# One-hot rows in one VectorE instruction, earlier negated means, and squares of incoming rows spread one, two, one: attention, routing and eight experts on one core

## What is computed

```python
x = x + jnp.tanh(g_xattn[0]) * attention(layernorm(x), ctx, ctx, lens, lens, W, b)
x = x + jnp.tanh(g_ffn[0]) * experts(layernorm(x), router_w, w_gate, w_up, w_down)

# attention: softmax(Q K^T / 16, masked) V W^T + b, with K = V = ctx, 77 rows per batch
# experts:
logits = xf @ router_w.T
routing = softmax(logits)
top_w, top_i = top_k(routing, 2);  top_w = top_w / sum(top_w)
g = einsum('nd,ehd->neh', xf, w_gate);  u = einsum('nd,ehd->neh', xf, w_up)
y = einsum('neh,edh->ned', silu(g) * u, w_down)
out = einsum('ned,ne->nd', y, combine)     # combine holds top_w at top_i
```

## Time and profile before

| | us |
|---|---|
| median of 3 runs | 419.22 |
| lowest and highest run | 418.49, 422.79 |
| the profiled execution | 420.82 |
| its span, first to last instruction | 419.1 |
| PE busy in the span | 406.4 |
| DVE busy | 311.4 |
| ACT busy | 287.4 |
| POOL busy | 280.6 |

### The profile page before, as it was taken

The page is one execution under the profiler, slowest core; times in us unless marked ns, Lnnn a source line. Parts: engine busy times, 40 slices in busy tenths (PEclk is TensorE's granted clock), DMA queues, the critical chain, the costliest instruction groups (busy, mean ns, idle before and its releaser), DMA issues.

```text
span 419.1 us, 9883 instructions
## 1 busy us (share of the span) xinstructions
PE 406.4 (97%) x3211; PEld 377.1 (90%) x3211; DVE 311.4 (74%) x690; ACT 287.4 (69%) x585; POOL 280.6 (67%) x271
## 2 busy tenths in 40 slices
PE   8999899989999999999999999999999999999993
PEld 3788676556999999999999999999999999999993
DVE  6579978985877677777777777867777777777772
ACT  2489876364767776767777676777676777777672
POOL 7007574647377667777776766776777777777775
PEclk9999969999999999999999999999999999999998
DMA  6948875654876777543433333343334343333333
GB/s 184 346 153 276 283 241 181 228 178 119 289 166 144 176 180 167 127 62 52 63 64 64 51 55 60 56 68 66 52 51 63 51 63 64 64 51 56 59 60 63
DMA packets 34625, 50.26 MB, mean 120 GB/s; under 512 B 3846, under 2 KB 26023, under 8 KB 34599
## 3 DMA queue, kind: packets, MB, share of 16 engines
q0 software_dynamic: 13440, 19.19, 27.4%
q1 hardware_dynamic: 19815, 29.84, 22.5%
q10 hardware_dynamic: 1344, 0.92, 0.7%
HBM read 32.24 MB, written 17.70 MB: 119 GB/s over the span
## 4 chain that ended last, share of the span: by engine, by line
PE 45%; POOL 24%; issue 16%; DVE 6%; DMA 3%; ACT 2%; POOLq 2%; SPq 0%; ACTq 0%; DVEq 0%
POOL out_rows L523 15%; PE GT L1269 11%; PE UP L1269 11%; PE Y L1297 10%; POOL xt L511 8%; PE W L1114 3%; PE S L1139 3%; PE O L1188 2%; PE XT L1259 2%; DMA xg<-in_x 2%; DVE xg L911 1%; DMA out_rows<-y,idx 1%; POOLq L60 1%; POOLq L540 1%; ACT ex L614 1%
## 5 line engine op out<-in xcount | busy, mean ns | idle before, releaser
L523 POOL DMA_INDIRECT out_rows<-y,idx x68 | 159.7, 2349 | 64.6 <-ACT y L685 51.1
L1057 DVE TENSOR_TENSOR gu<-raw,gu 128x1024 fp32r<-128x1024 f32 x70 | 85.8, 1226 | 62.7 <-ACT gu L661 58.4
L1269 PE MATMUL GT<-xtT,gu 128*128 128x256 f32 x828 | 113.4, 286 | 0.0
L1269 PE MATMUL UP<-xtT,gu 128*128 128x256 f32 x828 | 110.6, 283 | 0.0
L1269 PEld LDWEIGHTS UP<-xtT,gu 128*128 128x128 f32 x828 | 104.3, 192 | 0.0
L1269 PEld LDWEIGHTS GT<-xtT,gu 128*128 128x128 f32 x828 | 103.8, 191 | 0.1
L1297 PE MATMUL Y<-dn,hT 128*128 128x256 f32 x816 | 103.5, 283 | 0.0
L1297 PEld LDWEIGHTS Y<-dn,hT 128*128 128x128 f32 x816 | 100.4, 192 | 0.0
L511 POOL DMA_INDIRECT xt<-xn_rows,idx x74 | 75.2, 1017 | 27.4 <-issue 22.2
L661 ACT CAST gu<-raw 128x1024 fp32r x68 | 70.8, 1042 | 30.7 <-PE UP L1269 29.4
L1078 DVE TENSOR_TENSOR hid<-hid,UP 128x512 f32<-128x512 f32 x68 | 46.5, 684 | 9.7 <-PE UP L1269 9.7
(11 more groups left out here) (172 smaller groups left out, 396.8 us busy)
## 6 DMA issues: line engine op xcount, KB each, us to landing
raw<-in_weights SPq DMA_DIRECT2D x32, 384.0 KB
xn_rows<-pay SPq DMA_DIRECT2D x8, 528.0 KB, 3.4
xTg<-in_xT SPq DMA_DIRECT2D x8, 512.0 KB, 4.4
xg<-in_x SPq DMA_DIRECT2D x8, 512.0 KB, 6.2
out_rows<-xg SPq DMA_DIRECT2D x8, 512.0 KB, 4.1
xt<-xn_rows,idx POOLq DMA_INDIRECT x74
out_rows<-y,idx POOLq DMA_INDIRECT x68
kr<-in_ctx_rows SPq DMA_DIRECT2D x1, 308.0 KB
```

The costliest lines, as they stand in the source:

```text
L523: gp.indirect_dma_start(out=out, out_offset=bass.IndirectOffsetOnAxis(ap=idx[:, 2 * j + t:2 * j + t + 1], axis=0), in_=y[:, j % 2, t, :], ...
L1057: return tt(out=out, in0=whole, in1=high.bitcast(F32), op=ALU.subtract)
L1269: last = mm(bank[:, h * PT:(h + 1) * PT], gu[:, pw, q, c, w, h * P:(h + 1) * P], xtT[:, b, px, c], start=(h == 0 and c == 0 and n == 0), s ...
```

## The change

Four things change.

1. `at_low` is made by one instruction for each unit, which compares the row of places with the unit's place and multiplies by its code, both given as one number per partition. The four comparisons (L860) and the multiplication (L870) of a group go; eight of the new form stand where the comparisons stood, two at a place. `low` and `code` become float32, and `iota_p` and `at_low` lose the pairing, also for the last group on ScalarE and for the list product on TensorE.
2. On VectorE the negated means of group n + 1 move from behind `ve` to a place ahead of the maxima of group n.
3. On ScalarE the squares of group n + 1 were two behind `inverse_sqrt` and two behind the exponentials. Now one stands ahead of `inverse_sqrt`, two behind it, and one behind the exponentials. A wait on `ssq_ready` of an earlier group is added.
4. The unread products behind attention are 0, 2, 3, 5, 4, 5, 6 for k = 0 to 6 in place of 0 and six times 3, and those ahead of the counts are 18, not 22.

```diff
-        iota_p = sb("iota_p", [P, P, 2], F16, a)
+        iota_p = sb("iota_p", [P, P], F16, a)
...
-        at_low = sb("at_low", [P, UNITS // 2, P, 2], F16, a)
+        at_low = sb("at_low", [P, UNITS, P], F16, a)
...
             def sum_squares(g, tiles):
                 act.wait_ge(x_loaded[g % 3], 16 * (g // 3 + 1))
                 act.wait_ge(negmean_ready, g)
+                if g > 1:
+
+                    act.wait_ge(ssq_ready, g - 1)
...
                     sum_squares(n, tiles_of(n))
+
+                if n + 1 < GROUPS:
+                    sum_squares(n + 1, range(1))
                 inverse_sqrt(n)
                 if n + 1 < GROUPS:
-                    sum_squares(n + 1, front)
+                    sum_squares(n + 1, range(1, G - 1))
                 if n < GROUPS:
                     exponentials(n)
                 exp_gap(k)
                 if n + 1 < GROUPS:
-                    sum_squares(n + 1, back)
+                    sum_squares(n + 1, range(G - 1, G))
...
                 dve.wait_ge(places_ready, k + 1)
-                at = k * CU // 2
-                rows_hot[0] = mark(tt(out=at_low[:, at + lo // 2:at + hi // 2],
-                                      in0=iota_p[:].unsqueeze(1).to_broadcast([P, (hi - lo) // 2, P, 2]),
-                                      in1=by_two(low[:], k, lo, hi), op=ALU.is_equal))
-
-            def coded(k):
-
-                if k < 0:
-                    return
-                after(rows_hot[0])
-                of = at_low[:, k * CU // 2:(k + 1) * CU // 2]
-                tt(out=of, in0=of, in1=by_two(code[:].rearrange("p g c t -> p (g c t)"), k, 0, CU),
-                   op=ALU.mult).then_inc(low_ready, 1)
+                codes = code[:].rearrange("p g c t -> p (g c t)")
+                for u in range(k * CU + lo, k * CU + hi):
+                    last = ts(at_low[:, u], iota_p[:], low[:, u:u + 1], codes[:, u:u + 1], ALU.is_equal, ALU.mult)
+                if hi == CU:
+                    last.then_inc(low_ready, 1)
...
+                if n + 1 < GROUPS:
+                    negated_means(n + 1)
                 if more:
                     reduced = maxima(n)
                     router_part(n)
...
-                if n + 1 < GROUPS:
-                    negated_means(n + 1)
                 if k > 0:
                     low_places(k - 1, masked)
-                coded(behind)
                 refine(n)
...
+            BUSY = (0, 2, 3, 5, 4, 5, 6)
...
-                if k > 0:
-                    keep_busy(3, ET)
+                keep_busy(BUSY[k], ET)
...
-            keep_busy(22, W)
+            keep_busy(18, W)
...
-                last = mm(L[:, LIST:LIST + TILES], at_low[:, u // 2, :, u % 2], at_tile[:, u // 2, :, u % 2], start=(u == 0), stop=(u == UNITS - 1))
+                last = mm(L[:, LIST:LIST + TILES], at_low[:, u], at_tile[:, u // 2, :, u % 2], start=(u == 0), stop=(u == UNITS - 1))
```

More of the change, by code:

```diff
@@ L109, in moe_flamingo @@
         iota_e = sb("iota_e", [P, NE], F32, a)
-        iota_p = sb("iota_p", [P, P, 2], F16, a)
+        iota_p = sb("iota_p", [P, P], F16, a)
         iota_t = sb("iota_t", [P, TILES, 2], F16, a)
-        code = sb("code", [P, GROUPS, TOPK, G], F16, a)
+        code = sb("code", [P, GROUPS, TOPK, G], F32, a)
         code_last = sb("code_last", [P, 2, G], F32, a)
@@ L154, in moe_flamingo @@
         low_i = sb("low_i", [P, CU], I32, a)
-        low = sb("low", [P, UNITS], F16, a)
+        low = sb("low", [P, UNITS], F32, a)
         high = sb("high", [P, UNITS], I32, a)
@@ L452, in _ @@
             gp.iota(iota_e[:], [[1, NE]], base=0, channel_multiplier=0, **exact)
-            gp.iota(iota_p[:], [[1, P], [0, 2]], base=0, channel_multiplier=0, **exact)
+            gp.iota(iota_p[:], [[1, P]], base=0, channel_multiplier=0, **exact)
             gp.iota(iota_t[:], [[1, TILES], [0, 2]], base=0, channel_multiplier=0, **exact)
@@ L690, in _ @@
             for u in range(CU):
-                nc.scalar.activation(apart[:, u], iota_p[:, :, 0], ACT.Square, bias=low_last[:, u:u + 1], scale=-1.0
+                nc.scalar.activation(apart[:, u], iota_p[:], ACT.Square, bias=low_last[:, u:u + 1], scale=-1.0
                                      ).then_inc(apart_ready, 1)
@@ L694, in _ @@
                 act.wait_ge(apart_ready, u + 1)
-                last = nc.scalar.activation(at_low[:, (UNITS - CU + u) // 2, :, u % 2], apart[:, u], ACT.Relu,
+                last = nc.scalar.activation(at_low[:, UNITS - CU + u], apart[:, u], ACT.Relu,
                                             bias=code_last[:, 0, u % G:u % G + 1], scale=code_last[:, 1, u % G:u % G + 1])
@@ L845, in low_places @@
                 v.tensor_copy(low[:, k * CU:(k + 1) * CU], low_i[:]).then_inc(places_ready, 1)
-            rows_hot = [0]
-            def by_two(of, k, lo, hi):
-                return of.rearrange("p (u two) -> p u two", two=2)[:, k * CU // 2 + lo // 2:k * CU // 2 + hi // 2].unsqueeze(2
-                       ).to_broadcast([P, (hi - lo) // 2, P, 2])
             def at_lows(k, lo, hi):
@@ L992, in _ @@
             at_lows(last_group - 1, 4, 8)
-            coded(last_group - 1)
             share(last_group)
```

## The result

| | before | after |
|---|---|---|
| median, us | 418.86 | 430.81 |
| lowest and highest run, us | 418.05, 422.79 | 429.21, 432.45 |
| runs | 4 | 4 |
| the profiled execution, us | 420.82 | 429.21 |
| its span, us | 419.1 | 427.4 |

The changed kernel takes 1.028 times as long (95% interval 1.024 to 1.032), 12.0 us more. The forecast was 421.0 us with a range to 424.0, about the same: it is wrong. A fourth run of the kernel before (418.05) has moved its median from 419.22 to 418.86.

A forecast was written before the change was run, and what follows sets the result against it. A ring of VectorE and ScalarE in the eight groups ahead of PE's pairs was taken to set the time; terms summed to +2.0 us on the profiled 420.82, put rounded down onto the median 419.22: 421.0 us, range 417.4 to 424.0.

The forecast's parts named there:

- Where the clock stood: Groups ahead of the pairs: TensorE's lower clock was taken to come as before, in group 4; chance 0.50.
- Group 4 is PE's ... no change: Group 4's step, set by PE at the lower clock: 10.0 us from E to the next lg as now.
- E: The moment in a group when ScalarE's exponentials end; 45.2 us in group 3.
- The price of a one-hot row: VectorE's new one-instruction row of 128 elements with two scalars: estimated 0.16 us, eight of them 1.28 us.
- the ring: Each group's chain on VectorE and ScalarE: E to ve 4.1 us, ve to the next E 3.4 us.
- -0.4 for groups 5 to 7: Groups 5 to 7 ask for no means: they save 0.4 us behind ve and nothing ahead of it.
- -0.3 for the end: End of the last group: 1.44 us become 1.28, and 18 products let the counts come earlier; -0.3 us.
- The rival of slow rows: New row on VectorE takes one element at a time and loads two scalars, 0.25 us: +3.2, 424.2 us; chance 0.07.
- The early means: VectorE's wait for scores delays ve: +0.5, +0.85, +0.3, +0.8 us in groups 0 to 3, the last two with rows.
- The squares: ScalarE's first square ahead of the logarithm costs nothing; waiting for x adds at most 0.3 us, in group 2; no gain.
- The products: PE's gaps before the transposes grow anyway: 1.1 us in group 2, 1.6 in group 3, where 0.53 and 1.22 stood.
- The rival of an earlier fall: Clock falls from group 2's gap and stays down over two groups: +1.7 and +0.4, 423.1 us; chance 0.13.

The follow-up runs named there:

- held changed kernel: The changed kernel with unread products raised to 3, 3, 8, 12, 12, 9, 9 behind attention and 24 ahead of the counts: 425.38 us.
- held pair: The changed kernel and the kernel before, each with more unread products filling PE's gaps behind attention: 425.38 us and 417.97 us.

## Why the prediction was wrong

**Where the clock stood (failed).** The first part read one profiled execution and took its fall in group 4 as how the kernel runs. It was the rarer kind. Two steps rest on that. "Group 4 is PE's ... no change": at a full clock group 4 takes 7.54 us before and 8.60 after, a loss of 1.06 us that was counted as nothing. Even with the fall the loss was not nothing: from E to the next `lg`, "10.0 us as now", the changed kernel took 10.68 (58.19 to 68.87), and `lg` of group 4, forecast near 55.4 us, came at 58.45. And the difference was put onto a median that mostly has no fall, although the text forecast one for every run. The granted clock of the profiled execution beside the time of the others (420.82 against a median of 419.22) was there to be read.

**The price of a one-hot row (mis-sized term).** 0.16 us was taken for 128 elements and two scalars; it is 0.222. The nearest row was L751, 0.19 us with one scalar and 256 elements. The step from it took elements as dear and a second scalar as cheap: it is the other way round, 0.033 us for 128 elements and 0.060 for a scalar (0.19 - 0.033 + 0.060 = 0.22). By it the rows cost 4.5 us in the ring. The terms -0.4 for groups 5 to 7 and -0.3 for the end have the wrong sign: +1.19, +0.74 and +0.98. The forecast's "nothing ahead of it" did not follow even from its own price, by which eight rows take 1.28 us for 0.8. In groups 5 and 6 no wait for scores takes in a pair, so all eight count, 8 x 0.222 = 1.78 us for 0.8. At the end the last eight took 2.00 us (91.92 to 93.92), 0.25 each, where 1.28 was forecast and the old form had 1.44. The rival of slow rows (0.25 us, +3.2 us, chance 0.07), put off with "Nothing in the rows speaks for it", came nearest in the price. Half of that is luck: it had the operation take one element at a time, and 128 more elements cost 0.033 us, not 0.13.

**The early means (right, with one omission).** The wait came where it was forecast, 1.67 us in group 0. For groups 1 to 4 the forecast had 0.4 to 0.7. The timeline of DVE in the held changed kernel, whose waits are not mixed with a slow clock, has 0.72 in group 1 and 0.23 in groups 2 and 3:

```profile
34.00 0.16 DVE L797 TENSOR_SCALAR negmean<-S 128x4 f32<-128x4 f32 x1 [0.72 <-PE S L1126]
...
41.46 0.16 DVE L797 TENSOR_SCALAR negmean<-S 128x4 f32<-128x4 f32 x1 [0.23 <-PE S L1126]
...
58.66 0.16 DVE L797 TENSOR_SCALAR negmean<-S 128x4 f32<-128x4 f32 x1
```

In group 4, the last row, it has none. With the old rows, in the kernel of means and squares, groups 1 to 4 waited 0.71, 0.45, 0.44 and 0.51: the dearer new rows ahead of the means take up the rest of the wait. Group 1 was to lose 0.85 and lost 0.83. Group 0 was to lose 0.5 and lost 0.91: `ve` came 0.77 us later behind `lg`, exactly as forecast (5.44 for 4.67), but the first square now stands ahead of the logarithm, and `rt0v` comes 0.99 us behind `ve` instead of 0.69. That is most of the 0.32 by which the early means alone, with 0.59, lose less. Group 2 was to lose 0.3 and lost 0.60 (7.98 before, 8.58 held). Group 3 was to lose 0.8 with rows and lost 0.56 by the means and 0.63 by the rows.

**The squares (right in sign, reason incomplete).** No gain, as forecast. The clause that the first square costs nothing "where ve comes later than it" holds only because the early means make `ve` late. On their own they wait for means and for x and cost about 3 us.

**The products (right, and too small a thought).** "The products do not make up for the longer ring": so it was, with gaps of 1.36 and 1.86 us where 1.1 and 1.6 were forecast. That the new counts alone change nothing is shown. What was not asked is what gap k = 0 would have, which has no product and where the first fall came.

**The rival of an earlier fall (right kind, wrong place and size).** It named group 2's gap and 423.1 us, chance 0.13. In the profile the fall came in group 1, and a second one, from 59 to 73 us, in group 4, together 4.3 us in that execution against the held kernel.

**The sum.** Forecast +2.0, of which 1.8 were put onto the median. Measured +12.0: 3.4 for the means and squares (forecast about +2 to group 3, nothing in group 4), 4.5 for the rows (forecast near 0 net), less 0.5 between the sum of steps and the medians, and 4.5 for the clock (forecast 0). Between the two profiled executions, which both have falls, it is +8.4: 7.5 of ring and 0.9 of clock (4.3 for the change, 3.4 before, each against its held kernel). So the ring is the larger miss, and 2.5 of the clock's 4.5 come from the base: the profiled execution before had lost 3.4 us to the clock, the median before 0.9. The 4.5 is what is left over when the ring is taken off, not a second measurement; that the steps outside the falls (3, 5 and 6) agree to 0.1 us with the held ones speaks for it. That falls are more frequent in the changed kernel is shown by counts: four of four runs at 0.976 or less, 14 of 48 before at 0.984 or less. That the gaps bring them, and not the longer ring as such, is shown by the held changed kernel, which has the ring and no such run.

**What stays open.** What decides whether a gap of a given length lets the clock fall. The idle 0.67 us at 31 us was followed by a fall in the changed kernel and in the one with the squares alone, and in the profiles of "means and squares" and of "all but rows", at the same place and length, it was not. With the early means alone 0.35 us there was followed by one; in "means and squares" 1.68 us before the transposes at 55.16 was not. No run here tells what differs.

## What to carry to other kernels

Before a forecast, compare the profiled execution's granted clock and time with those of the other runs, so that the base of the sum is the kind of execution that the median stands for. Price an instruction by its operands as well as by its elements: on small tiles two scalars per partition cost more than the elements, and one instruction in place of two or of a large one can be dearer. When the chain ahead of TensorE gets longer, look at every gap it opens, and measure the chain with the gaps filled before anything is said of the clock.

## What the runs showed of the hardware

- VectorE, 16-bit tensor_scalar of 128 elements in SBUF: 0.102 us with constants, 0.162 with one scalar per partition, 0.222 with two. A second operation with a constant adds nothing; 128 more elements are 0.033 us.
- Runs of one and the same kernel differ in whether TensorE's clock falls from the upper to the lower of its two levels: 15 of 52 runs of the kernel before took 421.1 to 423.2 us, the others 417.5 to 419.9. The stretches at 1.2 GHz among the groups began at the end of PE gaps of 0.35 to 1.9 us or up to 2 us behind it. They lasted from 3.4 us (32.4 to 35.8 with the squares alone) to 14 us (53 to 67 with the rows alone); PE was busy all of 35 to 40 and of 65 to 70 us in the changed kernel. With the gaps filled by products that nobody reads, 14 of 14 runs of the held pair and 12 of 12 with the comparisons moved stayed at 0.993 or more. With the squares alone, which open a gap where the filling has no product, it was 8 of 10.
- Filling one gap and not the next showed no gain: 429.20 us for 430.81 with intervals that overlap, and in the profiles a fall at 47 us in place of those at 32 and 59.
